# A decoder block on one core: loads, first norm, projections and context transposes in another order

## The reference

```python
x = x + self_attention(layernorm(x), wq, wk, wv, wo)          # 32 query heads of 16, 8 key/value heads, causal
x = x + cross_attention(layernorm(x), ctx, mask, Wq, ...)     # 32 query heads of 128, 8 kv heads, RMS norm of q and k
x = x + ffn(layernorm(x), ...)
# ffn: relu(h @ up)**2 @ down, plus ((h @ fc1) @ expert) * (sum of the top two gate logits) @ fc2,
#      and a layernorm with gamma and beta over the sum
```

## Time and profile before

| | us |
|---|---|
| median of 3 runs | 1846.23 |
| lowest, highest | 1844.5, 1850.87 |
| profiled execution | 1853.32 |
| its span | 1851.6 |
| PE busy | 1733.9 (94%) |
| DVE, ACT, POOL busy | 941.9, 751.8, 650.7 |

### The profile page before, as it was taken

How to read it: one execution, slowest core, us unless ns; L and a number is a source line. 1 busy time by engine, 2 the same in 40 slices (tenths; PEclk the granted TensorE clock), 3 DMA queues, 4 the chain that set the end, 5 groups by cost and what they waited for, 6 DMA issues and landing times.

```text
span 1851.6 us, 29634 instructions
## 1 busy us (share of the span) xinstructions
PE 1733.9 (94%) x11352; PEld 1397.1 (75%) x11352; DVE 941.9 (51%) x1657; ACT 751.8 (41%) x1332; POOL 650.7 (35%) x511
## 2 busy tenths in 40 slices
PE   2989899999999999989949998999999999999898
PEld 1745678888888888878937557888888888887797
DVE  3169544444545544474450894545444445456654
ACT  1267444444443434431223763443434444434221
POOL 2188323242323332451012972322332322324410
PEclk8889999999999999999968998999999999999999
DMA  4110010110101101110041100101101101011100
GB/s 154 41 40 18 18 40 19 40 40 17 57 17 40 57 17 45 35 46 18 18 147 31 38 7 18 41 17 40 57 17 40 40 23 51 23 39 47 35 24 23
DMA packets 25871, 70.92 MB, mean 38 GB/s; under 512 B 3152, under 2 KB 3152, under 8 KB 25808
## 3 DMA queue, kind: packets, MB, share of 16 engines
q1 hardware_dynamic: 25808, 70.05, 12.2%
HBM read 65.85 MB, written 4.19 MB: 38 GB/s over the span
## 4 chain that ended last, share of the span: by engine, by line
PE 82%; DVE 6%; ACT 4%; POOL 3%; DMA 2%; issue 2%; SPq 0%; POOLq 0%; DVEq 0%
PE acc L358 14%; PE acc L359 13%; PE acc L360 13%; PE y L358 9%; PE y L360 8%; PE y L359 8%; PE acc L376 4%; PE sc L561 4%; PE ot L575 4%; PE pt L399 2%; ACT kt L850 2%; DMA kv<-in_ctx 2%; PE sc L489 1%; PE acc L544 1%; POOL prob L1371 1%
## 5 line engine op out<-in xcount | busy, mean ns | idle before, releaser
L1358 POOL TENSOR_TENSOR w_lo<-stage,w_hi 128x1024 fp32r<-128x1024 f32 (+1 forms) x88 | 171.2, 1956 | 310.5 <-ACT w_hi L721 310.5
L1371 POOL TENSOR_TENSOR prob<-prob,pmax 128x512 f32<-128x512 f32 x128 | 133.4, 1042 | 355.2 <-DVE pmax L1035 354.9
L358 PE MATMUL y<-w_hi 128*128 128x512 f32 x576 | 236.8, 411 | 0.9 <-issue 0.9
L358 PE MATMUL acc<-w_hi,xn_hi 128*128 128x512 f32 (+1 forms) x576 | 227.0, 394 | 2.9 <-DVE xn_lo L993 2.9
L360 PE MATMUL y<-w_hi,w_lo 128*128 128x512 f32 x576 | 225.7, 392 | 0.0
L359 PE MATMUL y<-w_lo,w_hi 128*128 128x512 f32 x576 | 224.7, 390 | 0.0
L360 PE MATMUL acc<-w_hi,xn_lo 128*128 128x512 f32 (+1 forms) x576 | 219.7, 381 | 0.0
L359 PE MATMUL acc<-w_lo,xn_hi 128*128 128x512 f32 (+1 forms) x576 | 219.5, 381 | 0.0
L993 DVE TENSOR_TENSOR w_lo<-ot,w_hi 128x1024 fp32r<-128x1024 f32 (+1 forms) x80 | 89.3, 1117 | 208.1 <-ACT w_hi L861 207.8
L1377 POOL TENSOR_TENSOR prob<-prob,prec 128x512 f32<-128x512 f32 x128 | 147.8, 1155 | 89.3 <-DVE prec L1043 89.3
L1362 POOL TENSOR_TENSOR qkrs<-qkve,mhalf 128x10 f32<-128x10 f32 x64 | 125.0, 1953 | 152.6 <-DVE qkve L1080 152.6
(11 more groups left out here) (129 smaller groups left out, 3685.8 us busy)
## 6 DMA issues: line engine op xcount, KB each, us to landing
stage<-in_w_cross SPq DMA_DIRECT2D x64, 512.0 KB, 3.6
stage<-in_w_cross SPq DMA_DIRECT2D x32, 256.0 KB, 2.7
stage<-in_w_ffn SPq DMA_DIRECT2D x16, 512.0 KB, 3.6
kv<-in_ctx SPq DMA_DIRECT2D x16, 256.0 KB, 3.4
x<-in_x SPq DMA_DIRECT2D x8, 512.0 KB, 7.0
stage<-in_w_self SPq DMA_DIRECT2D x8, 512.0 KB, 3.8
out_x<-x SPq DMA_DIRECT2D x16, 256.0 KB, 2.0
stage<-in_w_self SPq DMA_DIRECT2D x4, 256.0 KB, 7.7
```

The lines of the kernel that those rows point to most:

```text
L358: nc.tensor.matmul(target, l_hi, r_hi, start=first, stop=False)
L1358: nc.gpsimd.tensor_tensor(low, stage[:, place.slot(n), 0:width], high.bitcast(F32), ALU.subtract).then_inc(w_lo_done, 1)
L1371: nc.gpsimd.tensor_tensor(pr, pr, spread(pmax[:, buffer, :], 8, SEQ), ALU.subtract).then_inc(s_sub.sem, 1)
```

## The change

Nothing that is computed changes. What changes is the order, in five places.

1. SP: x and the self-attention weights are loaded first, then two context tiles, then the constants. The raw constants lie in `prob` and `probt` instead of `qb`; the context tiles lie in `kt` instead of `kv`.
2. Start of half 0: the norm of two tiles, their transposes and their keys and values follow one another, four times; the context transposes stand one behind each query product; the expert product comes after the last query.
3. End of half 0: SP interleaves stores of x with loads of x of half 1. PE transposes tiles 0 to 3 of half 1 inside the feed-forward chunks q = 2 and 3, the rest in `second_projections`.
4. POOL adds beta to all 8 tiles before the first result power, and stands its weight splits of half 1 between powers.
5. DVE in every feed-forward: `latent_lo(q + 1)` now comes after `result(2 * q + 1)`.

```diff
+FIRST = ("*ln0 *ln1 *kv0 *ln2 *ln3 *kv1 *ln4 *ln5 *kv2 *ln6 *ln7 *kv3 "
+         "*q0 *ctx0 *q1 *ctx1 *q2 *ctx2 *q3 *ctx3 *q4 *ctx4 *q5 *ctx5 *q6 *ctx6 *q7 *ctx7 " + SELF_END)
+BETWEEN = (FFN + " *ln0 *ln1 latt3 up30 up31 up32 up33 *ln2 *ln3 *ln4 *ln5 *kv0 *kv1 *kv2 *q0 *q1 *ln6 *ln7 *kv3 "
+           "*q2 *ctx0 *q3 *ctx1 *q4 *ctx2 *ctx3 *q5 *ctx4 *ctx5 *q6 *ctx6 *q7 *ctx7 " + SELF_END)
...
-        ctile = kv[:].rearrange("p t d -> p (t d)")[:, 0:2 * D].rearrange("p (r d) -> p r d", r=2)
         kt = sb("kt", [P, HALF])
+        ctile = kt[:].rearrange("p (r d) -> p r d", r=2)
...
+            place = Place(1, 1)
+            load_ctx(1, 0)
+            load_ctx(1, 1)
+            load_attention_pieces(place, w_self, (0, 1, 2))
+            for i in range(3):
+                store_x(0, i)
+                load_x(1, i)
+            load_attention_pieces(place, w_self, (3, 4, 5))
+            store_x(0, 3)
+            load_x(1, 3)
+            for i in range(2, NT):
+                load_ctx(1, i)
...
+            def self_kv(half, m):
+                at = Place(1, half).at
+                if m == 0:
+                    pieces_split(Place(1, half), 1)
+                for i in (2 * m, 2 * m + 1):
+                    evacuated(pe, at, A1[half][f"ln{i}"])
+                project_kv(at, A1[half][f"kv{m}"], m, xn_hi, xn_lo)
...
+            def first_projections():
+                for m in range(CHUNKS):
+                    first_norm(0, 2 * m)
+                    first_norm(0, 2 * m + 1)
+                    self_kv(0, m)
+                for n in range(NT):
+                    self_queries(0, n)
+                    transpose_ctx(0, n)
+                fold_experts()
+
+            def second_projections():
+                first_norm(1, 4)
+                first_norm(1, 5)
+                for m in range(3):
+                    self_kv(1, m)
+                self_queries(1, 0)
+                self_queries(1, 1)
+                first_norm(1, 6)
+                first_norm(1, 7)
+                self_kv(1, 3)
+                self_queries(1, 2)
+                transpose_ctx(1, 0)
...
                     down(q, 0)
+                    if q >= 2 and half == 0:
+                        first_norm(1, 2 * (q - 2))
+                        first_norm(1, 2 * (q - 2) + 1)
                     down(q, 1)
...
+            def second_projections():
+
+                place = Place(1, 1)
+                for n, m in ((0, 0), (1, 0), (2, 1)):
+                    act.wait_ge(acc_rdy.sem, Place(3, 0).at(acc_rdy, A3[0][f"up3{m}"] + 1))
+                    split_piece(place, n)
+                first_norm_hi(1, 2)
+                first_norm_hi(1, 3)
+                act.wait_ge(acc_rdy.sem, Place(3, 0).at(acc_rdy, A3[0]["up32"] + 1))
+                split_piece(place, 3)
...
+                    if q >= 2 and half == 0:
+
+                        i = 2 * (q - 2)
+                        first_statistics(1, i)
+                        first_statistics(1, i + 1)
+                        first_norm(1, i)
+                        first_norm(1, i + 1)
+                    if q == 3 and half == 0:
+                        first_statistics(1, 4)
+                        first_statistics(1, 5)
                     result(2 * q)
+                    if q >= 2 and half == 0:
+                        first_norm_lo(1, i)
+                        first_norm_lo(1, i + 1)
+                    if q == 3 and half == 0:
+                        first_norm(1, 4)
+                        first_norm(1, 5)
+                    result(2 * q + 1)
                     if q + 1 < CHUNKS:
                         latent_lo(q + 1)
-                    result(2 * q + 1)
...
+                for i in range(NT):
+                    beta_added(i)
+                for i in range(4):
+                    result_rsqrt(i)
+                if half == 0:
+                    later = Place(1, 1)
+                    layernorm_rstd(later.at, 0, 0)
+                    layernorm_rstd(later.at, 0, 1)
+                result_rsqrt(4)
+                result_rsqrt(5)
+                if half == 0:
+                    for n in range(3):
+                        split_piece(later, n)
+                    for i in range(2, 6):
+                        layernorm_rstd(later.at, 0, i)
+                result_rsqrt(6)
+                if half == 0:
+                    split_piece(later, 3)
+                result_rsqrt(7)
```

More of the change, by code:

```diff
@@ L340, in _, with store_x, load_cross_and_ffn @@
+            def store_x(half, i):
+                for t in (2 * i, 2 * i + 1):
+                    sp.wait_ge(x_out.sem, Place(3, half).at(x_out, t + 1))
+                    sp.dma_start(out[half, t], x[:, t, :]).then_inc(x_st[t].sem, 16)
+            def load_cross_and_ffn(half):
                 load_attention_pieces(Place(2, half, 0), w_cross[0], range(6))
@@ new lines, in second_projections @@
+            def second_projections():
[7 more added lines that the diff above has]
+                split_piece(place, 3)
+                first_norm_hi(1, 4)
+                first_norm_hi(1, 5)
+                for m in range(3):
+                    self_kv(1, m)
+                act.wait_ge(x_out.sem, Place(3, 0).at(x_out, NT))
+                self_queries(1, 0)
+                self_queries(1, 1)
+                first_norm_hi(1, 6)
+                first_norm_hi(1, 7)
+                self_kv(1, 3)
+                self_queries(1, 2)
+                ctx_hi(1, 0)
+                self_queries(1, 3)
+                ctx_hi(1, 1)
+                self_queries(1, 4)
+                ctx_hi(1, 2)
+                ctx_hi(1, 3)
+                self_queries(1, 5)
+                ctx_hi(1, 4)
+                ctx_hi(1, 5)
+                self_queries(1, 6)
+                ctx_hi(1, 6)
+                self_queries(1, 7)
+                ctx_hi(1, 7)
@@ L979, in last_turn_and_ffn @@
                     hidden_hi(q, 3)
+                    if q == 2 and half == 0:
+                        first_norm_hi(1, 0)
+                        first_norm_hi(1, 1)
                     if q + 1 < CHUNKS:
@@ L983, in _ @@
             for half in range(HALVES):
+                if half == 0:
+                    first_projections()
+                else:
+                    second_projections()
                 self_attention(half)
@@ new lines, in first_statistics, with first_norm, first_norm_lo, ctx_lo @@
+            def first_statistics(half, i):
+                at = Place(1, half).at
+                dve.wait_ge(x_ld[i // 2].sem, at(x_ld[i // 2], 1))
+                statistics(at, 0, i)
+            def first_norm(half, i):
+                normalise(Place(1, half).at, 0, i, A1[half][f"ln{i - 2}"] if i >= 2 else None)
+            def first_norm_lo(half, i):
+                layernorm_lo(Place(1, half).at, 0, A1[half][f"ln{i}"], i)
+            def ctx_lo(half, i):
+                transposed_lo(Place(1, half).at, A1[half][f"ctx{i}"], tile_of(cx_hi, i), tile_of(cx_lo, i),
+                              ctx_hi_done, i + 1)
@@ new lines, in first_projections @@
+            def first_projections():
+                first_statistics(0, 0)
+                first_statistics(0, 1)
+                for m in range(CHUNKS):
+                    first_norm(0, 2 * m)
+                    first_norm(0, 2 * m + 1)
+                    if m + 1 < CHUNKS:
+                        first_statistics(0, 2 * m + 2)
+                    first_norm_lo(0, 2 * m)
+                    first_norm_lo(0, 2 * m + 1)
+                    if m + 1 < CHUNKS:
+                        first_statistics(0, 2 * m + 3)
+                for i in range(NT):
+                    ctx_lo(0, i)
+                constants()
@@ L1066, in key_squares, with second_projections @@
+            def second_projections():
+                first_norm_lo(1, 4)
+                first_norm_lo(1, 5)
+                first_statistics(1, 6)
+                first_statistics(1, 7)
+                first_norm(1, 6)
+                first_norm(1, 7)
+                first_norm_lo(1, 6)
+                first_norm_lo(1, 7)
+                for i in range(NT):
+                    ctx_lo(1, i)
             def key_squares(place, k):
@@ new lines, in first_projections @@
+            def first_projections():
+                place = Place(1, 0)
+                at = place.at
+                layernorm_rstd(at, 0, 0)
+                layernorm_rstd(at, 0, 1)
+                split_piece(place, 0)
+                split_piece(place, 1)
+                for i in range(2, NT):
+                    layernorm_rstd(at, 0, i)
+                split_piece(place, 2)
+                split_piece(place, 3)
+                masks()
+                pool.wait_ge(f1g_hi_done.sem, 1)
+                nc.gpsimd.tensor_tensor(f1g_lo[:], f1g_raw, f1g_hi[:].bitcast(F32), ALU.subtract
+                                        ).then_inc(f1g_lo_done.sem, 1)
```

395 lines of the change are left out of this document (213 added, 182 removed).

## The result

| | before | after |
|---|---|---|
| median of the runs, us | 1846.22 (1844.5 to 1850.87) | 1808.47 (1807.23 to 1809.54) |
| ratio, 95% interval | | 0.9777 [0.9764, 0.9791] |
| profiled execution, us | 1853.3 | 1809.07 |
| span, us | 1851.6 | 1807.3 |

What follows compares the result with a forecast made beforehand. PE bounds most of the kernel, a chain of loads, transposes and copies the start and turn. Gains 17.2 and 21.5 less costs 1.1 and 0.8 give 36.8: 1846.2 to 1809 us, own range 1803 to 1816, 80% in 1797 to 1821.

Steps and rivals of the forecast that it cites:

- The start: Start of half 0 to its first scores: 79.4 us against 96.6, a gain of 17.2.
- the four rounds: Start of half 0, two norms and one key-value product each: end at 44.9 us if slow, 33.9 if fast.
- the fold: Start of half 0, the expert product, now behind the queries: 3.5 us.
- the clock is high early: Rival, start of half 0: clock high from the first product, gain 27.9 instead of 17.2, 1799 us; chance 0.22.
- slow queries: Rival, query stretches: 16 queries at 1.2 GHz, each 2.7 us more, 1861 us in all; chance 0.03.
- The wait ahead of tiles 2 and 3: The turn: PE waits about 2.2 us for these norms, whose powers stand behind POOL's splits.
- The result step beside the split: The turn: DVE's last step of result 6 waits for POOL's 2.34 us split, ending near 935.1 instead of 933.1.
- the key product at about 9 us after the last `down`: Sign of being right at the turn: half 1's first key product starts about 9 us after the last `down`.
- Rests behind the result: Feed-forward, `latent_lo` after the odd result: PE waits about 0.27 us, four times, 1.1 us.
- Additions in one go: Feed-forward, beta added on POOL all at once: costs 0.4 us in each half, 0.8 together.
- Loads don't come earlier: Rival, the turn: half 1's x loads held behind stores until the last result, 1823 us; chance 0.03.
- More waits at the turn: Rival: slips in POOL's list hold three engines; gain 28.2 us in all, 1818 us; chance 0.18.

Runs made afterwards that it cites:

- start_only: The changed kernel with half 1 prepared as in the kernel before, so only the start of half 0 is new there; 1826.87 us, ratio 0.988.
- turn_only: The changed kernel with half 0 started as in the kernel before, so the turn to half 1 stays changed; 1826.84 us, ratio 0.9878.
- after_again: The changed kernel run and profiled once more without an edit, on another chip; 1806.68 us, ratio 0.9767.
- pool_mend: The changed kernel with POOL's powers of tiles 2 and 3 ahead of three weight splits, the fourth split behind result 7's power; 1807.4 us, ratio 0.9778.
- norms_first: The changed kernel with all eight norms ahead of the keys and values in the start of half 0; 1810.38 us, ratio 0.9785.
- context_last: The changed kernel with the eight context transposes behind all queries in the start of half 0; 1811.85 us, ratio 0.9799.
- best1: pool_mend with old orders of latent rests and beta, rests of tiles 4, 5 before result 7, ACT's start splits before the key copy; 1799.9 us, ratio 0.9735.
- beta_as_before: The changed kernel with only the beta additions put back between the result powers; 1809.76 us, ratio 0.9781.

## Why the prediction was right, point by point

**The bound.** Two stretches bound by a chain: right. start_only and turn_only give 22.0 us each, and each moves its own stretch.

**The start.** The load, the norms and the first product were within 0.7 us (13.37 against 14). The clock was the term that was mis-sized. I had the four rounds end at 42.9 with 2 us off for one early rise; they ended at 38.8, because the clock was high from 17.9 on, within the first product, and fell to 0.50 only for 3.4 us near 28. The queries took 29.3 (29.8), the fold 3.44 (3.5), from there to the scores 2.8 (3.2). So the start, 74.4, lies between the forecast (79.4) and the rival *the clock is high early* (68.7), outside the 76 to 82 that the prediction names as a sign of being right. How many falls of the clock a start meets is not the order's doing alone: after_again has one (33.4 to 37.0) and 73.7, pool_mend with the same start two (22.0 to 25.6, 35.6 to 39.0) and 76.0. In norms_first the products that follow 18 us of transposes start at half speed too, 0.21 us apart, and in context_last the granted clock is 0.50 from 65 to 78, over transposes with waits for loads between them and the expert product behind them. The Trainium skill's rule (TensorE: Matmul & The Clock Gate, Part 4: PE-mode transpose), that transposes don't bring the clock up, agrees with these two. In both the engine also stood idle between transposes, and no run here parts the two causes. The prediction says that this rule is worked out in its second and third rivals; only the third, *slow queries*, has to do with it. In the changed start the clock came up within the first product all the same, and stayed up through most of the short transposes and waits, as in the stretch from 836 in the earlier trace rows. A small part was missed altogether: ACT's splits of pieces 2 and 3 (1.05 us each) stand ahead of the copies of the next tiles, and two of the three gaps are 3.64 instead of 3.0. In best1, where they stand ahead of the copy of the keys, the second gap is 3.01 (24.70 to 27.71); the third stays at 3.62, because PE waits 0.92 us for a norm there.

**The turn.** The wait ahead of tiles 2 and 3 was forecast at 2.2, for the reason given, and was 1.81 us. The result step beside the split was forecast to be blocked for the split, and took 2.83. From the last latent transposes to the first key product 33.1 us passed (34.4 forecast), from there to the scores 49.8 (47.8), with one fall of the clock to 0.50 for 3.4 us (918.8 to 922.4), for which I had allowed 1.0. One sign was given wrongly: the key product at about 9 us after the last `down`. That is the distance to 931.70, the end of the last `down` in the kernel before. By the prediction's own times it is 940.7 - 935.7 = 5.0, and 4.4 were measured (913.47 to 917.83). What I had not seen is that this wait and this step are only worth something together with the next one: pool_mend removes both and gains nothing that can be told, best1 moves the rests too and its turn is 5.4 us shorter.

**The rest.** Rests behind the result: 0.27 us each forecast, 0.23 measured, four times. Additions in one go: 0.4 in each half forecast, 0.7 measured. Together 1.9 and 2.3, as spacings; no difference of the runs or of the stretches is fine enough to confirm the sum. That the two depend on each other (beta_as_before) was not in the forecast.

**The sum.** 5 us too little in the start, and the kernel before, whose profiled execution was 7.1 us over its median, gave 44.3 by the profiles and 37.8 by the medians. On the other chips it was 42.7. That one profile of before overstates both stretches: against turn_only's start (93.5) and start_only's turn (102.8) the changed kernel is 19.1 and 19.9 us shorter, 41 together with the 1.0 us that each of them kept of the change. So 1809 against 1808.5 is in part luck: the gain was forecast some 5 us too small by what other chips measured, and the kernel before was 3 us faster on this chip than there.

**The rivals.** *Slow queries*: refuted, the clock is 1.00 from 38.80 to 74.38. *Loads don't come earlier*: refuted, tiles 0 to 5 of half 1 are transposed inside the feed-forward or right behind it, and PE waits 1.81 and 0.73 us for their norms. Only the fourth load of `x` is late, DVE waits 4.45 us for it until 922.74, but PE does not wait. *More waits at the turn*: not so, 82.9 us in place of the 83.2 forecast.

## What to carry to other kernels

A stretch in which no engine is busy is a chain, and here the cheapest cut was the order of the first loads: ask what stands ahead of it in the queue (11 of 22 us here, for moving nine loads of 1.8 MB in all). When a wait ends last on a chain of several engines, look up what would end second; an edit that removes one of two equal waits measures as nothing and is not refuted by that. Edits that look small and separate can share an instruction: price the pair (0.23 or 1.19 us for the same move). And before a difference of 2 us in one stretch is explained, profile the same kernel twice.

## What the hardware showed that was not expected

The granted clock of the first stretch, 0 to 13.37 and some us beyond, stands at 1.00 in the profile, while matmuls at 14.14 and 14.36 are 0.22 us apart, as at 0.50 in the earlier trace rows; from 17.9 on they are 0.12 apart. norms_first shows the same for longer: 1.00 from 8 to 31 us, and products 0.21 us apart up to 30.8. At the start of these executions the spacing of matmuls tells the clock, the row does not.

I had counted on a block by POOL only for DVE steps with two wide inputs. In best1 the application of a norm, which has one, took 1.50 us beside splits and 0.55 us before them (timelines of DVE and POOL):

```profile
898.56 0.55 DVE L1160 TENSOR_SCALAR xn<-x,mv,rstd 128x512 f32<-128x512 f32 x1
899.54 1.50 DVE L1160 TENSOR_SCALAR xn<-x,mv,rstd 128x512 f32<-128x512 f32 x1 [0.44 <-POOL rstd L1567]
...
899.48 5.06 POOL L1563 TENSOR_TENSOR w_lo<-stage,w_hi 128x512 fp32r<-128x512 f32 x3
```

The Trainium skill has this in SBUF — State Buffer, Who interferes with whom: an operation of this kind can run in a mode that takes the ports it shares with GpSimd. I had read only its line on two inputs; the row agrees with the other one.

Low stretches of the clock come and go between executions of the same kernel. Stretches of the changed kernel's two profiled executions behind the first scores, columns as in the earlier trace rows:

```profile
74.40:100.00 25.60, 22.88 (x96) 10.72 (x97) 15.78 (x29) 16.50 (x37) 22.01 (x18) 0.73 0.11 32
...
73.70:100.00 26.30, 21.00 (x113) 9.56 (x113) 18.38 (x35) 19.23 (x42) 25.60 (x21) 1.00 0.17 50
```

One had a granted clock of 0.55 from 74.4 to 88.1 and took 714.3 us from the first scores to the first latent transposes, the other had none of it and took 712.0. context_last had its low stretch ahead of the scores (0.51 from 64.9 to 78.6) and took 711.2. With one profile each, that looked like a stretch moved by the edit; the second profile of the same kernel shows that it need not be.
